# Delta stage in units of eight heads by 256 tokens, rows by transposition, GpSimd taking SBUF work from VectorE

## The reference

```python
q = causal_conv_silu(x @ Wq, ...)      # depthwise, 4 taps along time; same for k and v
g = -exp(A_log) * softplus(x @ Wfa @ Wfb + dt_bias)
beta = sigmoid(x @ Wb)
q = l2norm(q) * SCALE ; k = l2norm(k)
def step(S, inp):                      # lax.scan over time, S: 128 x 128 for each head
    S = S * exp(gt)[..., None]
    vd = (vt - einsum('bhkv,bhk->bhv', S, kt)) * bt[..., None]
    S = S + kt[..., None] * vd[:, :, None, :]
    return (S, einsum('bhkv,bhk->bhv', S, qt))
o = o * rsqrt(mean(o * o) + EPS) * o_norm_w * sigmoid(gate)
return o.reshape(b, t, D) @ Wo
```

## Time and profile before

| | |
|---|---|
| median of 3 runs | 3720.73 us (3720.51 to 3722.68) |
| profiled execution | 3717.97 us, its span 3715.8 us |
| PE busy | 3474.6 us (94%) |
| PE weight loads busy | 1694.5 us (46%) |
| DVE busy | 1941.4 us (52%) |
| ACT busy | 1427.4 us (38%) |
| POOL busy | 125.0 us (3%) |
| mean granted TensorE clock | 0.965 of 2.4 GHz |

### The profile page before, as it was taken

How to read it: one execution, slowest core, us unless ns; L and a number is a source line. 1 busy time by engine, 2 the same in 40 slices (tenths; PEclk the granted TensorE clock), 3 DMA queues, 4 the chain that set the end, 5 groups by cost and what they waited for, 6 DMA issues and landing times. The chain is left out here.

```text
span 3715.8 us, 86134 instructions
## 1 busy us (share of the span) xinstructions
PE 3474.6 (94%) x37416; PEld 1694.5 (46%) x37416; DVE 1941.4 (52%) x3334; ACT 1427.4 (38%) x3313; POOL 125.0 (3%) x457
## 2 busy tenths in 40 slices
PE   6979999996789999999999999999999759999999
PEld 4454444442344544444444444444444435444444
DVE  2131111113778897789878878887888431111111
ACT  1010000001466656666665666566656521000000
POOL 0000000000000000000000000000000000000000
PEclk9979999997989999999999999999999868999999
DMA  4011100003111111121111111111211042000000
GB/s 154 7 57 36 28 0 29 11 0 120 48 31 36 42 50 34 45 66 41 33 56 43 48 50 45 42 37 39 65 39 34 16 154 63 14 15 29 0 12 12
DMA packets 83725, 156.21 MB, mean 42 GB/s; under 512 B 8782, under 2 KB 33998, under 8 KB 79516
## 3 DMA queue, kind: packets, MB, share of 16 engines
q1 hardware_dynamic: 83356, 150.77, 12.3%
HBM read 133.71 MB, written 17.04 MB: 41 GB/s over the span
## 5 line engine op out<-in xcount | busy, mean ns | idle before, releaser
L1333 PE MATMUL psum<-dl_xt,dl_wqkv 128*128 128x512 f32 x1536 | 778.2, 624 | 10.4 <-DVE dl_qkv L977 10.0
L513 DVE SCALAR_TENSOR_TENSOR f_act_g<-psum,f_bup,f_act_g 128x512 f32<-128x512 f32 x96 | 72.1, 751 | 939.4 <-ACT f_act_g L468 939.4
L977 DVE SCALAR_TENSOR_TENSOR dl_qkv<-psum,dl_par,dl_qkv 128x511 f32<-128x511 f32 (+2 forms) x576 | 430.4, 747 | 14.0
L468 ACT ACTIVATE f_act_g<-psum,f_bgate 128x512 f32<-128x512 f32 x96 | 66.0, 687 | 923.1 <-PE psum L411 923.1
L1333 PEld LDWEIGHTS psum<-dl_xt,dl_wqkv 128*128 128x128 f32 x1536 | 257.4, 189 | 250.2 <-issue 212.5
L411 PE MATMUL psum<-xnt_sb,wup 128*128 128x512 f32 x768 | 345.2, 592 | 0.0
L407 PE MATMUL psum<-xnt_sb,wgate 128*128 128x512 f32 x768 | 345.2, 592 | 0.0
L429 PE MATMUL psum<-f_wdown,f_hidden 128*128 128x512 f32 x768 | 344.9, 592 | 0.0
L1340 PE MATMUL psum<-dl_wo,dl_sg 128*128 128x512 f32 x512 | 260.9, 623 | 2.9 <-DVE dl_qkv L977 2.5
L407 PEld LDWEIGHTS psum<-xnt_sb,wgate 128*128 128x128 f32 x768 | 145.9, 190 | 183.7 <-issue 183.7
L411 PEld LDWEIGHTS psum<-xnt_sb,wup 128*128 128x128 f32 x768 | 145.9, 190 | 183.7 <-issue 183.7
(11 more groups left out here) (192 smaller groups left out, 4618.1 us busy)
## 6 DMA issues: line engine op xcount, KB each, us to landing
dl_wqkv<-in_dw_qkv SPq DMA_DIRECT2D x192, 256.0 KB, 2.6
dl_wo<-in_dwo SPq DMA_DIRECT2D x16, 1024.0 KB, 5.2
f_weights_b<-f_weights_by_expert SPq DMA_DIRECT2D x48, 256.0 KB, 6.3
wgate<-in_wgate SPq DMA_DIRECT2D x2, 3072.0 KB, 18.6
wup<-in_wup SPq DMA_DIRECT2D x2, 3072.0 KB, 24.7
f_wdown<-in_wdown SPq DMA_DIRECT2D x2, 3072.0 KB, 13.6
x_sb<-in_x SPq DMA_DIRECT2D x4, 1024.0 KB, 9.3
x_after_experts<-x_sb SPq DMA_DIRECT2D x16, 256.0 KB, 2.0
```

The costliest lines, as they stand in the source:

```text
L977: tap_ = lambda dl: dve.scalar_tensor_tensor(y_[:, dl:TT], ps[:, bank, 0:TT - dl], par[:, h, 4 * a + 3 - dl:4 * a + 4 - dl], y_[:, dl:TT], ...
L1333: last = pe.matmul(ps[:, bank, :], wq[:, n % RING, m, :], xt[:, u // HG % 2, m, :], start=(m == 0), stop=(m == KC - 1))
```

## The change

The delta stage is laid out anew; the other stages stay. A unit is 8 heads by 256 tokens (2 units side by side for each 256 tokens, still 16 units), with 8 slots of two chunks in a row of heads each: 128 slots in all, with 8 matmuls instead of 4 in each state piece. The tensors lie as chunk, head, token instead of head, token.

- Each slot has 4 main jobs. A projection covers 256 tokens plus 3 tokens before them (259 columns), so the convolution needs no boundary; `tap` and the three taps of `convolve` have 256 elements, and there are 24 projections for each unit instead of 12. Output rows take their weights in quarters of 2 heads (`wo`, two buffers); the ring has 6 buffers.
- `by_rows` uses 4 transpositions of 128 by 128 for a job.
- All four job banks are shared by main and short jobs; each job takes the bank whose last job comes first in the order.
- A level is one piece; `late_tokens` does it on VectorE in three instructions (queries and keys together, early keys, decays).
- The softplus series (now on a buffer of its own and in six steps), `near_zero`, `decayed` and `o_scale` are on GpSimd, in a fixed order around the solve.
- ScalarE's list is reordered: taps and copies for "long" jobs come ahead of `take_u`.

```diff
-TT = 512
+HE = 2
+HU = HJ * HE
+TT = 256
+HALO = 3
+SLOTS = CH
+PROJ = 3 * HU
+RING = 6
+JOB_BANKS = (4, 5, 6, 7)
...
+    if sl in (3, 4):
+        jobs = [("rows", k - 1, i, q) for q in (2 * sl - 6, 2 * sl - 5) for i in range(RB)]
     else:
+        unit, first = {0: (k + 1, 8), 1: (k + 1, 12), 2: (k + 1, 16), 5: (k + 1, 20), 6: (k + 2, 0), 7: (k + 2, 4)}[sl]
+        jobs = [("proj", unit, first + n, 0) for n in range(4)]
...
+    table = {(0, "long"): [("vrow", k, 1)], (0, "inner"): [("vrow", k, 2)], (0, "split"): [("vrow", k, 3)],
+             (1, "inner"): [("gate", p, 0), ("gate", p, 1)], (1, "split"): [("gate", p, 2)], (1, "end"): [("gate", p, 3)],
+             (2, "long"): [("turn", p, 0), ("turn", p, 1)], (2, "inner"): [("turn", p, 2)], (2, "split"): [("turn", p, 3)],
+             (3, "states"): [("level", w, 0)], (3, "long"): [("level", w, 1)], (3, "end"): [("level", w, 2)],
+             (4, "states"): [("sums", w, 0)], (4, "long"): [("level", w, 3)], (4, "end"): [("level", w, 4)],
+             (5, "long"): [("level", w, 5)],
+             (6, "long"): [("krow", w, 0), ("dec", w2, 0)], (6, "inner"): [("krow", w, 1), ("dec", w2, 1)],
+             (6, "split"): [("dec", w2, 2)], (6, "end"): [("dec", w2, 3)],
+             (7, "states"): [("cross", w, 0)], (7, "long"): [("krow", w, 2)], (7, "inner"): [("krow", w, 3), ("corner", w, 0)],
+             (7, "end"): [("vrow", w, 0)]}
...
+    for job in order:
+        if job not in place:
+            bank = min(JOB_BANKS, key=lambda b: ends[b])
+            place[job] = (bank, used[bank])
+            used[bank] += 1
+            ends[bank] = last[job]
...
+                def series(u):
+                    pool.wait_ge(s["softplus_exp"], u + 1)
+                    if u > 0:
+                        pool.wait_ge(s["softplus_sum"], u)
+                    for n, c in enumerate((1.0 / 3.0, -0.5, 1.0)):
+                        if n == 0:
+                            pool.tensor_scalar(poly[:, :], all_w, -0.25, c, ALU.mult, ALU.add).then_inc(s["series"], 1)
+                        else:
+                            pool.wait_ge(s["series"], 6 * u + 2 * n)
+                            pool.tensor_scalar(poly[:, :], poly[:, :], c, None, ALU.add).then_inc(s["series"], 1)
+                        pool.wait_ge(s["series"], 6 * u + 2 * n + 1)
+                        pool.tensor_tensor(poly[:, :], poly[:, :], all_w, ALU.mult).then_inc(s["series"], 1)
...
+                for k in range(-2, UNITS + 1):
...
+                    if prep:
+                        near_zero(w)
+                    if post:
+                        o_scale(p)
+                    if prep:
+                        decayed(w, QQ)
+                        decayed(w, KK)
+                        solve(w)
+                    if ahead:
+                        series(w2)
...
+                def late_tokens(u, lv):
...
+                    dve.tensor_tensor(late, late, dv[:, :, 0, 0:1].unsqueeze(1).broadcast_to([P, 2, nb, m]),
+                                      ALU.mult).then_inc(s["late"], 1)
...
+                    dve.tensor_tensor(keys, keys, dv[:, :, 1, 0:1].broadcast_to([P, nb, m]), ALU.mult).then_inc(s["early_keys"], 1)
+                    dve.wait_ge(s["late"], LEVELS * u + lv)
+                    dve.tensor_tensor(dv[:, :, 0, 0:1], dv[:, :, 0, 0:1], dv[:, :, 1, 0:1], ALU.mult).then_inc(s["left"], 1)
...
+                    done_before = {0: [(w, 7), (w, 8), (w, 9)], 1: [(w, 11), (w, 12), (w, 13)], 2: [(w, 15), (w, 16), (w, 17)],
+                                   3: [(w, 19)], 4: [], 5: [(w, 20)], 6: [(w, 22), (w, 23), (w2, 0), (w2, 1)],
+                                   7: [(w2, 3), (w2, 4), (w2, 5)]}
+                    done_behind = {0: [(w, 10)], 1: [(w, 14)], 2: [(w, 18)], 3: [], 4: [], 5: [(w, 21)], 6: [(w2, 2)], 7: [(w2, 6)]}
...
                         if run:
                             add_state(k, sl)
+                        if sl == 5 and prep:
+                            whole_decay(w)
+                        if sl in (3, 4, 5) and prep:
+                            level_take(w, 2 * sl - 5)
+                        if sl == 1 and prep:
+                            choose(w)
+                        if sl == 4 and prep:
+                            turn_beta(w)
+                            norm_tables(w)
+                        if sl == 5 and prep:
+                            blocks_out(w)
+                        convolutions(done_behind, sl)
+                        if sl == 2 and post:
+                            gated(p, 0)
+                            gated(p, 1)
...
                 def by_rows(bank, src, n):
                     for m in range(4):
-                        for j in range(HJ):
-                            last = pe.matmul(ps[part(j), bank, P * m:P * m + P], chunk(src, g0 + m)[:, j, :], ident,
-                                             start=True, stop=True)
+                        g = CH * (m // 2) + 2 * n + m % 2
+                        last = pe.transpose(ps[:, bank, P * m:P * m + P], src[:, g].rearrange("p j t -> p (j t)"), ident)
...
+                        all_main(main[0:2])
                         all_short(k, sl, "long")
                         if run:
                             solve_u(k, sl)
                         all_short(k, sl, "inner")
+                        all_main(main[2:3])
                         if run:
                             state_step(k, sl)
                         all_short(k, sl, "split")
+                        all_main(main[3:4])
                         all_short(k, sl, "end")
```

More of the change, by code:

```diff
@@ L564, in short_jobs @@
+    once = {(1, "end"): ("beta", w, 0), (3, "split"): ("ga", w, 0), (4, "split"): ("fa", w2, 0)}.get((sl, at))
     jobs = [once] if once and once[1] % HG == 0 else []
-    if 7 <= sl <= 10 and at in ("inner", "end"):
-        jobs.append(("level", w, sl - 5, first if at == "inner" else second))
-    jobs += table.get((sl, at), [])
-    return [(j[:3], j[3]) for j in jobs if 0 <= j[1] < UNITS]
+    return [j for j in jobs + table.get((sl, at), []) if 0 <= j[1] < UNITS]
 def place_jobs():
-    used, place = [0] * 8, {}
@@ L574, in place_jobs @@
[L574 to L580 removed]
+    order = []
     for k in range(-2, UNITS + 1):
         for sl in range(SLOTS):
[L583 to L588 removed]
+            main = [j for j, _ in main_jobs(k, sl)]
+            order += short_jobs(k, sl, "states") + main[0:2] + short_jobs(k, sl, "long") + short_jobs(k, sl, "inner")
+            order += main[2:3] + short_jobs(k, sl, "split") + main[3:4] + short_jobs(k, sl, "end")
@@ L589, in place_jobs @@
+    last = {job: n for n, job in enumerate(order)}
+    ends, used, place = {b: -1 for b in JOB_BANKS}, {b: 0 for b in JOB_BANKS}, {}
+    for job in order:
[4 more added lines that the diff above has]
+            ends[bank] = last[job]
     return place
@@ L878, in inverse_norms, with shorts, taps @@
                     act.activation(f, f, ACT.Exp, scale=-0.5).then_inc(s["roots"], 1)
+                def shorts(k, sl, at):
+                    for job in short_jobs(k, sl, at):
+                        if job[0] not in ("level", "turn", "sums", "cross", "corner"):
+                            short(job)
+                def taps(jobs):
+                    for job, _ in jobs:
+                        if job[0] == "proj":
+                            tap(*job[1:])
                 for k in range(-2, UNITS + 1):
@@ L934, in _ @@
-                        if sl == 6 and prep:
-                            act.wait_ge(s["k_silu"], w + 1)
-                            act.activation(by_tokens(kkt(w)), qkv[:, KK], ACT.Square).then_inc(s["k_square"], 1)
-                        for at in ("long", "inner"):
-                            for job, _ in short_jobs(k, sl, at):
-                                if job[0] not in ("level", "turn", "cross", "corner"):
-                                    short(job)
-                        job = main_job(k, sl)
@@ L942, in _ @@
-                        if job and job[0] == "proj":
-                            tap(*job[1:])
-                        for job, _ in short_jobs(k, sl, "end"):
-                            if job[0] not in ("level", "turn", "sums", "cross", "corner"):
-                                short(job)
-                        if sl == 9 and prep:
-                            inverse_norms(w)
             @block.vector
@@ L1217, in _ @@
[L1217 to L1228 removed]
+                        if sl == 2 and post:
+                            o_factor(p)
@@ L1342, in long_job @@
-                    if 3 in parts:
-                        last.then_inc(full[bank], 1)
-                def by_rows(bank, src, g0):
+                        if q == 0:
+                            for e in range(HE):
+                                wait_read(pe, "turn", u, HE * i + e)
+                        if i == 0:
+                            pe.wait_ge(wo_in[q % 2], 16 * (2 * u + q // 2 + 1))
```

(11 more changed lines are left out.)

798 lines of the change are left out of this document (358 added, 440 removed).

## The result

| | before | after |
|---|---|---|
| median | 3720.62 us (3714.07 to 3722.68, 4 runs) | 3998.47 us (3990.77 to 4013.11, 4 runs) |
| profiled execution, span | 3715.8 us | 4001.9 us |
| mean granted TensorE clock | 0.965 | 0.921 |

The ratio is 1.0755 (95% interval 1.0718 to 1.0791). The change costs 278 us; the forecast said 12, and the range ended at 3830.

A forecast was written before the change was run, and what follows sets the result against it. TensorE was taken as the bound: 112.1 us of work plus 14.0 of waits make a unit 126.1. Fourteen units +15, last unit -8, start +5: +12 on 3717.97, 3730 profiled, 3733 as median; range 3630 to 3830.

The forecast's parts named there:

- GpSimd's time for its one-operation instructions: GpSimd's 2048-element steps in series and near_zero: 2.3 us with one input, 4.1 with two; series 20 us.
- gate 0: ScalarE's gate in slot 1, wanting the series' buffer at 19.6 us; GpSimd ends 19 us into the unit, nothing lost.
- TensorE's own work: TensorE's matmul work in each unit of the delta stage: 9.1 us less, so 112.1 us.
- waits for other engines: TensorE's waits in each unit, made by the new order of the engines' lists: 14.0 us against 3.8 before.
- the start of the stage: Start of the delta stage, the same chain with the slower GpSimd in it: +5 us.
- turn 3: Slot 2: needs turn 0's bank, freed by gated behind add_state and a convolution: TensorE waits 3.7 us.
- projection 0: Next unit's projection, needing the bank of projection 21, whose convolution VectorE runs late, slots 5 to 6: 4.6 us.
- Projection 16: Slots 1 to 2: needs the bank of projection 14, whose convolution stands behind choose: TensorE waits 2.0 us.
- Rival 2: GpSimd too late for gate 0, series from 22 us: +56, 3789; collisions +35, 3768; chance 0.17 including collisions.
- a rival with 0.11: TensorE at half the clock behind two waits a unit, each costing 4 us: +112, 3845; chance 0.11.
- The prediction's own sign of being wrong: Granted clock below 0.97 in the steady part; also no waits at turn 3 and projection 0, or 259-column records over 0.24 us.
- Levels, cross and corner in one piece each: -0.8: TensorE term for each unit: fewer entries into pieces, 0.1 us an entry, 0.8 us saved.

The follow-up runs named there:

- best3: both with level 0 between main jobs, cross behind the state step of slot 7 and blocks_out behind slot 6's convolutions: 3760.06 us, ratio 1.0110.
- both: The changed kernel with a second operation in the series' two additions and VectorE's list reordered: 3769.31 us, ratio 1.0142.
- none_pool: The changed kernel, reordered, with all of GpSimd's new work back on VectorE, spread over slots 0 to 3: 3901.23 us, ratio 1.0478.
- two_ops: The changed kernel with a do-nothing second operation in GpSimd's two series additions and the near_zero comparison: 3905.67 us, ratio 1.0494.
- both_thin: both with three quarters of each projection's weight transfer after the first six left out: 3761.26 us, ratio 1.0099.

## Why the prediction was wrong

The forecast was 3733 us with a range to 3830, the result 3998.47. Three steps of the prediction failed: GpSimd's time for its one-operation instructions, which made it late at gate 0; the lower clock, put at nothing; and TensorE's stalls, which were in no term. By size the clock comes first.

| a unit, us | predicted | measured |
|---|---|---|
| TensorE's own work | 112.1 | 112.4 (the unit of best3, clock 0.99) |
| waits for other engines | 14.0 | 17.5 (140.0 / 8) |
| stalls | 0 | 5.7 (45.9 / 8) |
| lower clock | 0 | 9.1 (972.11 / 8 - 112.4) |
| unit | 126.1 | 144.75 |

The 15 units up to the start of the last took 273.6 us more, the start of the stage 24.7 more, the rest of the span 12.2 less: 286.1, the difference of the spans. The prediction had +15 for 14 units, +5 for the start and -8 for the last unit, so the start was missed by some 20 us as well; in the run both it is only 6.3 us later than in the kernel before (first keys_state at 1057.2 us instead of 1050.9), so most of that has the same causes. The slots of a unit took 12.4, 23.6, 20.6, 18.1, 16.8, 15.4, 19.7 and 18.2 us on average, where 12, 15, 19, 15, 15, 13, 19 and 15 were forecast. (Matmul records are missing here and there, so the split between work and idle time is good to about 1 us a unit.)

- **TensorE's work** was right, in sum and in parts: by_rows went from start to start in 0.49 to 0.58 us, 8 records of 259 columns took 1.92 less their entry, the state pieces 0.46 to 0.66 each.
- **VectorE**: 94.6 us a unit instead of 87, no bound, as said. Part of the difference is time that its instructions stood behind GpSimd's (corner_in's last step 2.9 us, 0.7 in none_pool).
- **Waits**: turn 3 3.6 us (28.9 / 8; 3.7 forecast), projection 0 3.5 (4.6), level 0 0.9 (1.0), cross 1.0 (0.6). Projection 16, for which 2.0 stood, did not wait in the unit read; 17 did, 0.7. With GpSimd in time, slot 1 took the 15 us of the forecast in the units without beta (15.4 in two_ops).
- **GpSimd is the step that failed first.** "I take 4.1 with two inputs, 2.3 with one", and the series "is then 20 us". Two inputs took 4.5, one input with two operations 1.9, but one input with one operation 5.5, above the upper bound of 4.9; nothing in the trace before had that form. The series took 27.0 (inside its bounds of 11 to 29), near_zero ended 32.4 us after the start of the series, and gate 0's place, "nothing lost, and nothing to spare", turned into 4.4 us a unit (35.4 / 8). Rival 2 had the place right, and its threshold of 22 us lies between the series of two_ops, 20.1 us with no such wait, and the 27.0 here; it was given 0.17 with collisions. With a second operation in the two additions alone 93 us went.
- **The clock** was counted against with one row, 3.29 us of idling followed by 3.70 us for 8 records. One such case at the full clock did not exclude the others: here too some waits of 3.0 to 3.3 us left the clock alone, but all 27 of 3.5 us and more were followed by the lower one. It should have been a term of the sum as soon as the walk gave two waits above 3 us, and not a rival with 0.11. Its size there, 4 us for each wait, was too high: 9.1 us for the two forecast waits, the one by GpSimd and the stalls, some 2 us for each. The prediction's own sign of being wrong, a granted clock below 0.97 in the steady part, came true with 0.91.
- **The stalls** were in no term and no rival. The prediction welcomed "Levels, cross and corner in one piece each: -0.8"; that edit made the runs of 128. The stalls are 5.7 us a unit, and part of the clock's loss stands behind them; cutting the runs took two thirds of them away, but no run turned that into time.
- **Collisions** were put at 2.5 us a unit on TensorE. In the kernel before the same amount of GpSimd work cost 7; how much of the 17.5 is theirs in the new layout was not measured by itself.
- **Weight traffic** at nothing was right (both_thin: -8 us of 3769).

The single causes, each taken away alone: the additions' form -93, VectorE's order -109, the clock (by filling the waits) -90. They overlap, since each takes part of the clock's loss with it. Even with the first two edits together (the run both) the time is 36 us above the forecast, although the long waits before turn 3 and projection 0, which the forecast counted at 8.3 us a unit, are gone from it; that it lies inside the range is no merit of the prediction's mechanism.

## What to carry to other kernels

Where a forecast finds recurring waits of TensorE of the length seen here (3.5 to 5.1 us, and some of 3.0 to 3.3), price each with the stretch at half the clock behind it, and ask whether cheaper work could fill it; here the two edits together gave 229 us, and 93 and 109 alone. Before work is moved to GpSimd, time the very form of each instruction (one or two operations, comparison or addition), and count VectorE's instructions with two SBUF inputs beside it, small ones too. Short matmuls issued in long unbroken runs can stall TensorE; keep longer matmuls between them, but not at the price of a result that another engine waits for.

## What was not expected of the hardware

- GpSimd's tensor_scalar on 2048 elements: 1.90 us with (mult, add), 2.0 with (add, mult), 5.5 with add alone, 5.4 with is_lt alone, 7.1 with (is_lt, mult). At 1024 elements, add alone took 2.95 us and (mult, add) 1.04. A second operation that does nothing makes the addition 2.7 times as fast, and the comparison slower. Why, no run shows.
- Stalls of TensorE of up to 3.9 us with no engine shown that it waited for, 92 of them in a kernel that had none, by nothing but 64 short matmuls more in each run.
- A load on GpSimd alone, on a buffer of its own, slowed a kernel bound by TensorE by 2.9%.
